# Routing in three pair steps and seven groups, and shorter tile tables, in a graph, attention and experts layer

## The reference

```python
xn = layernorm(x)
x  = x + gnn(xn, src, dst) + linear_attention(xn)     # all 6250 rows, 256 columns
f  = layernorm(x)
p  = softmax(relu(f @ router_w1 + router_b1) @ router_w2 + router_b2)   # 6 experts
top_w, top_i = top_k(p, 2);  w = softmax(top_w)
y_e = relu(relu(f @ w1[e] + b1[e]) @ w2[e] + b2[e]) @ w3[e] + b3[e]
x  = x + sum over the two chosen experts of w * y_e
```

## Time and profile before

| what | value |
|---|---|
| median of 3 runs | 802.78 us (802.03 to 805.83) |
| the profiled execution | 807.41 us, span 805.6 us |
| busy shares | PE 84%, PEld 78%, DVE 69%, ACT 55%, POOL 50% |
| mean granted TensorE clock | 0.936 |
| stage 2 in the trace | about 286 to 420 us |
| no matmul of TensorE between | 428 and 449 us |
| first tile of stage 3 on ScalarE | 448.13 us |

### The profile page before, as it was taken

The page is one execution under the profiler, slowest core; times in us unless marked ns, Lnnn a source line. Parts: engine busy times, 40 slices in busy tenths (PEclk is TensorE's granted clock), DMA queues, the critical chain, the costliest instruction groups (busy, mean ns, idle before and its releaser), DMA issues.

```text
span 805.6 us, 15446 instructions
## 1 busy us (share of the span) xinstructions
PE 679.5 (84%) x4744; PEld 625.0 (78%) x4744; DVE 557.4 (69%) x1401; ACT 442.0 (55%) x873; POOL 398.9 (50%) x439
## 2 busy tenths in 40 slices
PE   3867999999999678878861599999994799999992
PEld 2867888888888567777741499999994799999992
DVE  5676579898888557767746277677773377777772
ACT  2545566777777236756740466556651566565640
POOL 3436378877666000443637045555555145555553
PEclk9989999999999799999955699999998699999997
DMA  8784645444443434764234434343432524545420
GB/s 230 158 166 119 158 126 142 134 126 140 128 121 87 155 118 143 238 191 155 71 99 129 121 117 140 130 140 133 131 120 84 166 88 127 147 124 137 134 73 29
DMA packets 72463, 106.24 MB, mean 132 GB/s; under 512 B 24612, under 2 KB 45605, under 8 KB 72386
## 3 DMA queue, kind: packets, MB, share of 16 engines
q1 hardware_dynamic: 51074, 72.57, 31.9%
q0 software_dynamic: 21312, 32.69, 13.4%
HBM read 60.32 MB, written 46.78 MB: 133 GB/s over the span
## 4 chain that ended last, share of the span: by engine, by line
PE 76%; ACT 6%; DVE 5%; DMA 4%; issue 4%; POOL 3%; SPq 1%; POOLq 0%; DVEq 0%; ACTq 0%
PE kv_ps L1303 10%; PE kv_ps L1305 10%; PE kv_ps L1304 10%; PE pt L1295 6%; PE d_ps L1174 5%; PE kv_ps L1151 5%; PE kv_ps L1154 4%; PE kv_ps L1152 4%; PE kv_ps L1238 3%; PE xt_ps L1295 3%; POOL tab L553 2%; PE pt L1229 2%; PE pt L1154 2%; PE pt L1151 2%; PE pt L1152 2%
## 5 line engine op out<-in xcount | busy, mean ns | idle before, releaser
L1303 PE MATMUL kv_ps<-we_h,now_h 128*128 x648 | 198.1, 306 | 13.9 <-issue 8.3
L1305 PE MATMUL kv_ps<-we_h,now_l 128*128 x648 | 185.5, 286 | 0.0
L1304 PE MATMUL kv_ps<-we_l,now_h 128*128 x648 | 184.9, 285 | 0.0
L1303 PEld LDWEIGHTS kv_ps<-we_h,now_h 128*128 128x128 f32 x648 | 125.6, 194 | 19.6 <-issue 19.6
L1304 PEld LDWEIGHTS kv_ps<-we_l,now_h 128*128 128x128 f32 x648 | 125.4, 194 | 0.0
L1305 PEld LDWEIGHTS kv_ps<-we_h,now_l 128*128 128x128 f32 x648 | 124.7, 193 | 0.0
L1099 DVE TENSOR_TENSOR work<-kv_ps,be 128x256 f32<-128x256 f32 x216 | 81.6, 419 | 45.0 <-PE kv_ps L1305 41.1
L564 POOL TENSOR_TENSOR arena<-work,arena 128x256 f32<-128x256 f32 x80 | 53.1, 683 | 109.2 <-ACT work L730 109.2
L524 POOL DMA_INDIRECT alg<-al_tab,src_all x50 | 62.1, 1243 | 41.9 <-issue 28.1
L914 DVE TENSOR_REDUCE ss<-xring 125x16 f32<-125x1040 f32 x50 | 61.7, 1234 | 20.3 <-ACT xring L635 17.7
L527 POOL DMA_INDIRECT arena<-xt_tab,dst_all x50 | 61.8, 1236 | 15.2 <-issue 15.2
(11 more groups left out here) (238 smaller groups left out, 1832.1 us busy)
## 6 DMA issues: line engine op xcount, KB each, us to landing
arena<-tab SPq DMA_DIRECT2D x40, 259.0 KB
xring<-in_x SPq DMA_DIRECT2D x26, 224.0 KB
xt_tab<-arena SPq DMA_DIRECT2D x10, 568.8 KB
arena<-tab SPq DMA_DIRECT2D x40, 131.0 KB
we_h<-wt_h SPq DMA_DIRECT2D x6, 768.0 KB
we_l<-wt_l SPq DMA_DIRECT2D x6, 768.0 KB
weight_in<-tab SPq DMA_DIRECT2D x14, 259.0 KB
xring<-in_x SPq DMA_DIRECT2D x5, 560.0 KB
```

The source lines that it names most:

```text
L1303: pe.matmul(outp, hi[:, c, :], we_h[:, w], start=c == 0, stop=False)
L1304: pe.matmul(outp, hi[:, c, :], we_l[:, w], start=False, stop=False)
L1305: last = pe.matmul(outp, lo[:, c, :], we_h[:, w], start=False, stop=c == KC - 1)
```

## The change

It has four parts.

1. **Three pair steps.** Of a group that ends at pair R, parts 1 and 2 of `route` are both run in step R + 3, the second Exp in R + 3, `ranks` and part 3 in R + 4. The loops have 29 steps, not 31.
2. **Seven groups** of 5, 5, 4, 4, 3, 2, 2 pairs, which end at pairs 4, 9, 13, 17, 20, 22, 24.
3. **Last steps reordered.** ScalarE normalises the last pair ahead of the Relu of pair 23, and TensorE transposes it ahead of the logits of pair 23.
4. **Tile tables.** The number of tiles is a rounding of the count (multiply, add, add and subtract 2^23). Ends are prefix sums over a zero-padded tile in three steps. The row of a tile is a weighted sum (region size less 128 times tiles of the experts passed, plus 128 j). Each k takes seven steps. Expert numbers have a semaphore of their own (`e_done`), and the engines wait for it at the start of each k.

```diff
-SIZES = (4, 5, 5, 4, 4, 3)
+SIZES = (5, 5, 4, 4, 3, 2, 2)
...
-        nmul = sb("nmul", [1, NM])
-        ntl = sb("ntl", [1, 2, EP])
+        jjs = sb("jjs", [1, NTT])
+        pad = 4
+        nrm = sb("nrm", [1, 2, 2, EP])
+        scan = sb("scan", [1, 3, 2, pad + EP])
+        ntl = scan[:, 0, :, pad:pad + EP]
         ends = sb("ends", [1, 2, EP])
+        coef = sb("coef", [1, 2, E])
...
-            pool.iota(nmul[:, :], pattern=[[S, NM]], base=0, channel_multiplier=0,
+            pool.iota(jjs[:, :], pattern=[[S, NTT]], base=0, channel_multiplier=0,
...
             def step(i):
+                if i == PR:
+                    normal2(i - 1)
                 if 0 <= i - 2 < PR:
...
+                    relu(i - 2)
                 if i < PR:
...
+                    stdev2(i)
+                    if i > 0:
+                        normal2(i - 1)
                 if 0 <= i - 1 < PR:
...
+                    evict2(i - 1)
...
-                if i - 4 in ROUTE:
-                    b = ROUTE[i - 4]
+                if i - 3 in ROUTE:
+                    b = ROUTE[i - 3]
                     n = 2 * SIZES[b]
                     act.wait_ge(d_ready, b + 1)
                     act.activation(tw[:, 5, 0:n], tw[:, 4, 0:n], ACT.Exp).then_inc(ex3_done, 1)
 
-            for i in range(PR + 6):
+            for i in range(PR + 4):
                 step(i)
 
-            act.wait_ge(tab_done, 2)
...
             for k in range(2):
+                act.wait_ge(e_done, k + 1)
...
             link(dve.tensor_copy(base[0:1, :, :], ebase[0:1, :, :]))
+            link(dve.memset(scan[:, :, :, :], 0.0))
...
-                for part in reversed(range(4)):
-                    if i - 2 - part in ROUTE:
-                        route(ROUTE[i - 2 - part], part)
+                for part, lag in ((3, 4), (1, 3), (2, 3), (0, 2)):
+                    if i - lag in ROUTE:
+                        route(ROUTE[i - lag], part)
...
-            ce = cnt[:, :, :].rearrange("p k e -> p (k e)")
-            nc_v = ncmp.rearrange("p k e m -> p (k e) m")
-            tlink(dve.tensor_tensor(nc_v, bc(ce, NM), nmul[:, :].unsqueeze(1).to_broadcast([1, 2 * EP, NM]), ALU.is_gt))
-            tlink(dve.reduce_sum(ntl[:, :, :].rearrange("p k e -> p (k e)"), nc_v, axis=AX.X))
-
-            tlink(dve.tensor_copy(ends[:, :, 0:1], ntl[:, :, 0:1]))
-            for e in range(1, E):
-                tlink(dve.tensor_tensor(ends[:, :, e:e + 1], ends[:, :, e - 1:e], ntl[:, :, e:e + 1], ALU.add))
+            tlink(dve.tensor_scalar(nrm[:, 0, :, :], cnt[:, :, :], 1.0 / S, (S - 1) / (2.0 * S), ALU.mult, ALU.add))
+            tlink(dve.tensor_scalar(nrm[:, 1, :, :], nrm[:, 0, :, :], float(1 << 23), None, ALU.add))
+            tlink(dve.tensor_scalar(ntl, nrm[:, 1, :, :], -float(1 << 23), None, ALU.add))
+            tlink(dve.tensor_scalar(coef[:, :, :], ntl[:, :, 0:E], -float(S), float(REG), ALU.mult, ALU.add))
+            for level in range(3):
+                to = scan[:, level + 1, :, pad:pad + EP] if level < 2 else ends[:, :, :]
+                back = pad - (1 << level)
+                tlink(dve.tensor_tensor(to, scan[:, level, :, pad:pad + EP], scan[:, level, :, back:back + EP], ALU.add))
 
             for k in range(2):
                 tlink(dve.tensor_tensor(ge[:, k, :, :], bc(jj[:, :], E), ends[:, k, 0:E].unsqueeze(1).to_broadcast([1, NTT, E]), ALU.is_ge))
-...
+                tlink(dve.tensor_tensor(gn[:, k, :, :], ge[:, k, :, :], coef[:, k, :].unsqueeze(1).to_broadcast([1, NTT, E]), ALU.mult))
+                tlink(dve.reduce_sum(tf[:, 0, k, :], gn[:, k, :, :], axis=AX.X))
+                tlink(dve.tensor_tensor(tf[:, 1, k, :], tf[:, 0, k, :], jjs[:, :], ALU.add))
+                dve.tensor_scalar(tab_row[:, k, :], tf[:, 1, k, :], float(E * REG), None, ALU.min).then_inc(tab_done, 1)
+                tlink(dve.reduce_sum(tf[:, 2, k, :], ge[:, k, :, :], axis=AX.X))
+                dve.tensor_scalar(tab_e[:, k, :], tf[:, 2, k, :], float(E - 1), None, ALU.min).then_inc(e_done, 1)
...
-            for i in range(PR + 6):
+            for i in range(PR + 4):
                 if 0 <= i - 2 < PR:
                     hidden(i - 2)
-                if i - 5 in ROUTE:
-                    ranks(ROUTE[i - 5])
+                if i == PR:
+                    turn_rows(i - 1)
+                if i - 4 in ROUTE:
+                    ranks(ROUTE[i - 4])
                 if i + 1 < PR:
                     mix(i + 1)
                 if 0 <= i - 2 < PR:
                     logits(i - 2)
-                if 0 <= i - 1 < PR:
+                if 1 <= i < PR:
                     turn_rows(i - 1)
```

More of the change, by code:

```diff
@@ L284, in gps_layer @@
         we_in, be_in, b3_in = sem("we_in"), sem("be_in"), sem("b3_in")
-        cnt_done, tstep, tab_done, fill_out = sem("cnt_done"), sem("tstep"), sem("tab_done"), [sem(f"fill_out{k}") for k in range(2)]
+        cnt_done, tstep, tab_done, e_done, fill_out = sem("cnt_done"), sem("tstep"), sem("tab_done"), sem("e_done"), [sem(f"fill_out{k}") for k in range(2)]
         fill_ready = sem("fill_ready")
@@ L673, in _, with relu, stdev2 @@
             act.activation(mix_h, xt_ps[:, :].rearrange("p (c n) -> p c n", c=KC), ACT.Copy).then_inc(mh_done, 1)
+            def relu(i):
+                act.wait_ge(rh_done, i + 1)
+                act.activation(rhT[:, :], rh_ps[:, 0:2 * P], ACT.Relu, bias=rb1_sb[:, 0:1]).then_inc(rhT_done, 1)
+            def stdev2(i):
+                part = slice(i % 2 * 2, i % 2 * 2 + 2)
+                act.wait_ge(ag2_done, 2 * i + 2)
+                act.activation(sd[:, part], mv[:, part, 1], ACT.Sqrt, bias=eps_sb[0:P, 0:1]).then_inc(sd2_done, 1)
@@ new lines, in normal2 @@
+            def normal2(i):
+                g, q = group_of(i), i % 2
+                act.wait_ge(fin2_done, 2 * i + 2)
+                if i >= 2:
+                    act.wait_ge(t2_done, i - 1)
+                for h in range(2):
+                    row = xr[g % RB][:, 2 * i + h - tiles_of(g)[0], :]
+                    act.activation(xnr[:, q, h, :], row[:, 0:D], ACT.Identity, bias=row[:, C_NMR:C_NMR + 1],
+                                   scale=row[:, C_R:C_R + 1]).then_inc(xn2_done, 1)
@@ L675, in step, with evict2 @@
+            def evict2(i):
+                act.wait_ge(t2_done, i + 1)
+                act.activation(xTr[:, :, :, 0:P], quad(pt[i % 2])[:, :, :, 0:P], ACT.Copy).then_inc(xT2_done, 1)
             def step(i):
+                if i == PR:
+                    normal2(i - 1)
                 if 0 <= i - 2 < PR:
-                    act.wait_ge(rh_done, i - 1)
-                    act.activation(rhT[:, :], rh_ps[:, 0:2 * P], ACT.Relu, bias=rb1_sb[:, 0:1]).then_inc(rhT_done, 1)
+                    relu(i - 2)
@@ L1082, in _ @@
-                tlink(dve.tensor_scalar(tf[:, 3, k, :], ge[:, k, :, E - 1], -1.0, 1.0, ALU.mult, ALU.add))
-                tlink(dve.tensor_tensor(tf[:, 4, k, :], tf[:, 2, k, :], tf[:, 3, k, :], ALU.mult))
-                tlink(dve.tensor_scalar(tf[:, 5, k, :], tf[:, 4, k, :], float(S), None, ALU.mult))
-                tlink(dve.scalar_tensor_tensor(tf[:, 6, k, :], tf[:, 0, k, :], float(REG), tf[:, 5, k, :], ALU.mult, ALU.add))
-                tlink(dve.tensor_scalar(tf[:, 7, k, :], tf[:, 0, k, :], float(E - 1), None, ALU.min))
```

27 lines of the change are left out of this document (6 added, 21 removed).

## The result

The changed kernel took 797.21 us (median of 15 runs, 795.81 to 808.75), the kernel before 803.83 (15 runs beside them, 801.05 to 808.06): ratio 0.9932 [0.9906, 0.9958]. Forecast were 794.7 and a range of 790.5 to 800. (The ratios here are estimated from all runs but those more than 1.5% above their kernel's fastest one, not from the medians, so they differ a little from the quotient of the medians.) The runs of the changed kernel fall into two groups, ten of 795.8 to 797.9 and five of 802.9 to 808.8, and these five show the lower granted TensorE clock, 0.929 to 0.940 over the run (about 0.945 in the others).

What follows compares the result with a forecast made beforehand. It took a backlog of scatters to bound the gap before the experts; SyncE would go on at 435.7 instead of 443.80 us, -8.1, subtracted from the median 802.78: 794.7 us, range 790.5 to 800 for 8 in 10.

Steps and rivals of the forecast that it cites:

- What ends the gap: Gap before the experts: a backlog of scatters ends it now; afterwards fills or the last scatter, SyncE going on at 435.7 us.
- Last steps: From eviction of pair 23 to the last logits: extra switch and new ranks paid by overlap, 0, bounds -1.5 to +3.
- The serial rival: Last steps: Relu, ranks and logits wait for each other at the low clock, +2 to +3 us, 797.5; chance 0.16.
- Counts, first fill: After `base` at 426.2 us: counts 0.8 later, the first fill of skip rows 1.5 after that, at 428.5.
- Fills: Six fills of skip rows before the experts: SyncE free of them 7.14 us after the first one's issue, at 435.65.
- Last scatter: GpSimd, group 6: last scatter starts at 430.9 against 439.93 us, -9.0, and lands at 434.8 to 436.9.
- the first rival: Gap's end: last scatter lands alone and fills are quicker, -9.0 us, 793.8; chance 0.60 together with the forecast.
- Tables: Tile tables on VectorE after the counts: 3.6 us, covered by 5 us of waiting for fills, so 0.
- The added lengthened round: Routing rounds up to pair 23: ten lengthened rounds instead of nine, +1.36 us, eviction at 410.67 rather than 409.31.
- The rivals of VectorE: Routing round with two parts: VectorE becomes the bound, 1.68 us in each of five groups, no change, 803; chance 0.08.
- the doubled switch: Routing rounds: a switch stops ScalarE for twice its load, 2.56 us more than the term, 797.3; chance 0.02.
- The clock: Routing rounds: TensorE falls to 1.2 GHz in one round per group, five groups lose 15 us, 809.7; chance 0.05.

## Why the prediction was right

- **What ends the gap.** Right. The backlog is gone (GpSimd idles before both last groups), fills and the last scatter end it. The tail is 29.8 to 30.6 us, forecast 29.3. (A slip of arithmetic that changes nothing: (439.93 - 420.42)/13 is 1.50, not 1.494.)
- **Last steps.** Right: from pair 23 to `base` 15.6 us, forecast 15.5. The serial rival (+2 to +3) is out.
- **Counts, first fill.** 0.8 and 1.57 us (1.54 in the second profile), as put.
- **Fills.** Mis-sized: 7.75 and 8.43 us for 7.14. The old figure was inferred from a wait put down to a scatter. Most of what is added lies in the issue (3.95 and 4.18 us for 3.36); neither dividing it over two queues nor doubling the stores told why.
- **Last scatter.** Issued `base` + 4.95 (4.7 put), landed 4.9 and 5.5 us later, in the bounds of 3.87 to 6.0. It is level with the fills, so two conditions end the gap, as in the first rival; but that rival had both early (793.8), and both are late.
- **Tables.** 3.9 us instead of 3.6, hidden; the run with the old ones says so.
- **The added lengthened round.** Right: 5.65 and 5.62 us one behind the other. The rivals of VectorE (+1.68 a group) and of the doubled switch are out. The Trainium skill's drain behind each table load ("ScalarE: Activation LUTs", section "What ACT_TABLE_LOAD costs") is not to be seen in these rounds: Exp starts 0.01 us behind the end of the 1.28 us load. By its 2.66 us a switch a pair costs 5.3 (an estimate by that page), here it costs 5.65 - 4.29 = 1.36.

```profile
320.53 1.28 ACT L718 ACT_TABLE_LOAD   x1
321.82 0.27 ACT L718 ACTIVATE lg<-lg 125x80 f32<-125x80 f32 x1
```

- **The size.** Forecast -8.1 us; measured -6.6 and -5.8 in medians, -5.9 with the clock held in both kernels. Two terms would make most of the difference. The fills' and scatter's 0.6 to 1.3 us is one (`base` to SyncE free of both: 10.1 and 10.7 us for 9.45). The other is a start too high: with the clock held, the tail of the kernel before is 37.5, 1.3 below its profile's 38.82, all of it between pair 23 and `base` (16.91 for 18.25). I took 443.80 from a profiled execution of 807.41 us and subtracted from the median of the others, saying that nothing in the sum belonged to the difference; these 1.3 us probably do. No trace of a typical run of the kernel before (near 802.8) was taken, so this second term is argued. With the clock held in both the tails agree with the times: 37.50 - 30.26 = 7.2, less the 1.36 of the added round 5.9 (in these two traces the rounds themselves differ by 2.7 us, for the extra matmuls lengthen five of them in the changed kernel and four in the one before, and two plain ones of the changed kernel are long). That the time came out 2.5 us above the point forecast has a third part: the kernel before itself measured 803.83 beside it, 1.05 more than the 802.78 from which I subtracted.
- **The clock.** I gave it 0.05 as the case of the median. It isn't that, but it is no rarity: 8 of 26 runs of the unaltered changed kernel lie at 802.6 or above, at the lower clock, and the profile has four low rounds (decisive from three on, I wrote; they ate the whole gain there). The place was only half right: the second of two paired lengthened rounds, twice in the profile above and three times in the run with the steps alone, but the very first round in both too, and once a plain round. Of three variants of the changed kernel with extra matmuls in the rounds none of 17 runs lies there; of the kernel before with them, 2 of 12 lie at 802.7 and 804.4. That fits TensorE's pauses as the cause without proving it: variants without extra matmuls have from none of 9 (old sizes) to 6 of 12 (old tables) above 802. Whether the three steps make it more frequent isn't settled: the kernel before has runs from 799.4 to 808.5 on the same chips.

## What to carry to other kernels

When a queue's backlog is taken away, what comes second sets the gain: find its row, and take its duration with its neighbours running beside it, since the two ends will now coincide. Before two profiled spans are compared, compare the granted clock by stage; here two equal spans hid a tail 9 us shorter behind rounds 9 us longer, most of that the clock. And run parts of a change beside the whole on one chip: where a kernel's runs spread over 10 us, ratios near 0.993 can't tell a part from the whole. Where TensorE pauses between rounds, matmuls of no use can be worth as much as the tuning of the work itself (5.2 us here, beside 5.8), if they last until the work resumes.

## What the runs showed of the hardware that was not expected

- The same program has executions with spans of 792.3 and 805.6 us; 11.2 of the 13.3 us lie in the rounds, 11.0 of them in four rounds in which the granted clock fell.
- The last scatter of 125 rows lands 3.9 us after its start with no store beside it and 4.9 to 5.5 with six stores under way; splitting the six over two queues changed nothing (11.07 us for 10.87 and 11.53), nor did twelve stores in place of six make it land later (5.1).
- In the run where the extra matmuls ended at 431.6, 4.5 us ahead of the first rows, the granted clock was 0.52 and 0.50 from 435 to 445 us. Where they lasted until the work it was 1.00, and the sixth tile came 1.9 us sooner.
